# DMA transposes that read HBM scratch in place of transposes out of SBUF, in a layer of gated scan attention and quantized feed-forward

## The reference

```python
xn  = (x - mean(x)) / sqrt(var(x) + 1e-5)                 # over the 1024 features
# gated scan, all [4096, 1024]
g, v, d = xn @ Wg + bg, xn @ Wv + bv, xn @ Wd + bd
xs, a   = sigmoid(g) * tanh(v), 0.001 + 0.998 * sigmoid(d)
h[t]    = a[t] * h[t-1] + xs[t]                            # over the tokens
# feed-forward with quantized operands, INNER = 4096
aq(t) = clip(round(t * s), -128, 127) / s,  s = 127 / max|t| of the row
wq(w) = clip(round(w * s), -1, 1) / s,      s = 1 / mean|w| of the whole matrix
ff    = aq(silu(aq(xn) @ wq(w_gate).T) * (aq(xn) @ wq(w_up).T)) @ wq(w_down).T
out   = x + h + ff
```

## Time and profile before

| | us |
|---|---|
| median of 3 runs | 7357.5 (7346.43 to 7358.31) |
| the profiled execution | 7350.78 |
| its span on the slowest core (6) | 7349.2 |
| spans of all cores | 7302.0 to 7349.2 |
| PE busy | 1947.6 (27%) |
| DVE busy | 3103.3 (42%) |
| ACT busy | 396.1 (5%) |
| chain that ended last: DVE / SP's queue / DMA / PE | 39% / 26% / 11% / 11% |

### The profile page before, as it was taken

The page is one execution under the profiler, slowest core; times in us unless marked ns, Lnnn a source line. Parts: engine busy times, 40 slices in busy tenths (PEclk is TensorE's granted clock), DMA queues, the critical chain, the costliest instruction groups (busy, mean ns, idle before and its releaser), DMA issues.

```text
span 7349.2 us, 43474 instructions; the slowest of 8 cores (7302.0 to 7349.2 us)
## 1 busy us (share of the span) xinstructions
PE 1947.6 (27%) x9490; PEld 975.5 (13%) x9490; DVE 3103.3 (42%) x5413; ACT 396.1 (5%) x676; POOL 16.2 (0%) x34
## 2 busy tenths in 40 slices
PE   0031312222130000000000054435344444535656
PEld 0021212112120000000000021112121111212222
DVE  2333334242334332332423267676676767631011
ACT  1010101011010000000000000000000000000000
POOL 0000000000000000000000000000000000000000
PEclk9965656666665555555555577777777777767878
DMA  4111101011113113211311111111111111147777
GB/s 86 51 36 26 35 26 35 26 35 29 34 27 123 40 49 115 78 48 51 109 41 48 41 27 31 36 35 31 37 30 36 31 36 31 35 148 238 246 247 239
DMA packets 575298, 496.12 MB, mean 68 GB/s; under 512 B 424448, under 2 KB 440864, under 8 KB 566848
## 3 DMA queue, kind: packets, MB, share of 16 engines
q1 hardware_dynamic: 571392, 486.92, 22.2%
q0 software_dynamic: 3648, 6.41, 0.6%
HBM read 339.86 MB, written 83.89 MB: 58 GB/s over the span
## 4 chain that ended last, share of the span: by engine, by line
DVE 39%; SPq 26%; DMA 11%; PE 11%; issue 8%; ACT 2%; DVEq 2%; POOL 0%; ACTq 0%; POOLq 0%
SPq L225 23%; PE pb L715 6%; DVE qt L196 3%; DMA wqg<-scr_wdT 3%; DVE qg L208 3%; DVE qnd L206 3%; DVE qt L210 3%; DVE qnd L211 3%; DVE pbuf L629 3%; DVE qg L449 2%; DVE qg L199 2%; DVE qcm L201 2%; DVE scal L639 2%; DVE pqstage L202 2%; PE pb L379 2%
## 5 line engine op out<-in xcount | busy, mean ns | idle before, releaser
L600 PE MATMUL pb<-wqg,xqF_t 128*128 128x512 bf16 x2048 | 846.0, 413 | 1780.6 <-DMA xqF_t<-scr_xqF 1603.8
L604 PE MATMUL pb<-wqu,xqF_t 128*128 128x512 bf16 x2048 | 844.2, 412 | 0.0
L379 PE MATMUL pb<-wqu,wqg 128*128 128x256 bf16 x3072 | 388.9, 289 | 1634.4 <-DMA wqu<-pqstage 1634.4
L715 PE MATMUL pb<-wqg 128*128 128x512 bf16 x2048 | 479.4, 398 | 424.2 <-DMA wqg<-scr_wdT 424.1
L379 PEld LDWEIGHTS pb<-wqu,wqg 128*128 128x128 bf16 x3072 | 311.1, 103 | 1689.2 <-issue 1637.7
L196 DVE TENSOR_SCALAR qt<-pbuf,wsc 128x512 f32<-128x512 f32 x192 | 93.3, 486 | 1029.8 <-DMA pbuf<-wdown 339.6
L600 PEld LDWEIGHTS pb<-wqg,xqF_t 128*128 128x128 bf16 x2048 | 214.3, 105 | 2110.5 <-issue 1918.2
L397 DVE TENSOR_TENSOR epi<-epi 128x256 f32<-128x256 f32 x128 | 54.4, 425 | 818.9 <-ACT epi L394 811.7
L421 PE MATMUL pb<-scal,ones_sb 128*1 128x1 f32 x6 | 0.6, 163 | 1422.3 <-DVE scal L452 1422.3
L733 DVE TENSOR_SCALAR qt<-pb,dpwall 128x512 f32<-128x512 f32 x64 | 48.0, 751 | 743.8 <-PE pb L715 727.0
L715 PEld LDWEIGHTS pb<-wqg 128*128 128x128 bf16 x2048 | 206.2, 102 | 697.4 <-issue 483.4
(11 more groups left out here) (80 smaller groups left out, 1929.3 us busy)
## 6 DMA issues: line engine op xcount, KB each, us to landing
wqg<-scr_wdT SPq DMA_DIRECT2D x512, 256.0 KB, 5.0
pbuf<-wdown SPq DMA_DIRECT2D x64, 512.0 KB, 4.8
pbuf<-wgate SPq DMA_DIRECT2D x64, 512.0 KB, 4.6
pbuf<-wup SPq DMA_DIRECT2D x64, 512.0 KB, 4.6
scr_pqF<-pqstage SPq DMA_DIRECT2D x32, 1024.0 KB, 4.1
wqg<-scr_pqF SPq DMA_DIRECT2D x32, 1024.0 KB, 8.3
pbuf<-x SPq DMA_DIRECT2D x32, 512.0 KB, 3.5
x_grp<-x SPq DMA_DIRECT2D x32, 512.0 KB, 4.5
```

Of the source, the lines that this page charges most:

```text
L379: e.matmul(o, l, r, start=st, stop=sp),
L600: e.matmul(o, l, r, start=st, stop=sp),
L604: e.matmul(o, l, r, start=st, stop=sp),
L715: e.matmul(o, l, r, start=st, stop=sp),
```

## The change

All transposes other than those of the gate's product now read a scratch tensor in HBM and write SBUF. Four edits belong together:

- Attention: xn and xq, untransposed, are stored to scr_xn and scr_xq after quantizing (four stores). SP waits for the xn stores and issues eight transposes of scr_xn, each [256 tokens, 128 features] to 128x256. xq is not transposed here, and the eight stores of scr_xqF are gone.
- Weights: each quantized chunk is stored to scr_wd, scr_wg or scr_wu at once; there are no batches. After all three weights, SP issues eight transposes of [4096, 128] for gate and eight for up. w_down is not transposed here, and scr_wdT is gone.
- Gate/up: the eight loads of a tile's xq are transposes of [128, 128] out of scr_xq.
- Down: each of the 32 pieces of w_down per pair is a transpose of [1024, 128] out of scr_wd, so w_down is transposed anew for each of the 16 pairs.

```diff
-            for kp in range(4):
-                k = 2 * kp
-                emit_xpose4([xnbf(0 * D + k * 128, 128), ...], xnF(k * GRP, 512), src_wait=srcw)
-            for kp in range(4):
-                k = 2 * kp
-                emit_xpose4([pqstage[:, 0 * D + k * 128:0 * D + (k + 1) * 128], ...],
-                    xqF(k * GRP, 512), src_wait=srcw)
+            vq_done = wv(V)
+            for tt in range(2):
+                rows = g * GRP + tt * 128
+                op("y", lambda e, i_=xnbf(tt * D, D), o=scr_xn[rows:rows + 128, :]:
+                   e.dma_start(out=o, in_=i_), sem=SN, inc=16, wait=(vq_done,))
+                op("y", lambda e, i_=pqstage[:, tt * D:(tt + 1) * D],
+                   o=scr_xq[rows:rows + 128, :]:
+                   e.dma_start(out=o, in_=i_), sem=SX, inc=16)
...
+            for k in range(8):
+                op("y", lambda e, o=xnF(k * GRP, GRP),
+                   i_=scr_xn[g * GRP:(g + 1) * GRP, k * 128:(k + 1) * 128]:
+                   e.dma_start_transpose(o, i_), sem=TD[k], inc=16,
+                   wait=tuple(xn_rd_wait) if k == 0 else ())
...
-            for k in range(8):
-                op("y", lambda e, i_=xqF(k * GRP, GRP), o=scr_xqF[k, :, g * GRP:(g + 1) * GRP]:
-                   e.dma_start(out=o, in_=i_), sem=SX, inc=16,
-                   wait=xpose_marks_g if k == 0 else ())
...
+            for li, (src_slice, dst_rows) in enumerate(load_list):      # prep_quant
+                buf = wchunk[li % 4]
+                lp = LP[li % 4]
+                lw_ = (vmarks[li - 4],) if li >= 4 else (wv(V),)
+                op("y", lambda e, o=buf, i_=src_slice: e.dma_start(out=o, in_=i_),
+                   sem=lp, inc=16, wait=lw_)
...
+                vmarks[li] = wv(V)
+                op("y", lambda e, i_=qtmp4(li % 4, 0, D), o=dst_rows:
+                   e.dma_start(out=o, in_=i_), sem=SWs[li % 4], inc=16,
+                   wait=(vmarks[li],))
...
+        for k in range(8):
+            op("y", lambda e, o=wqg[:, k * INNER:(k + 1) * INNER],
+               i_=scr_wg[:, k * 128:(k + 1) * 128]:
+               e.dma_start_transpose(o, i_), sem=WT, inc=16,
+               wait=(st_wg + (last_attn_T,)) if k == 0 else ())
...
-                   i_=scr_xqF[k, :, i * 128:(i + 1) * 128]:
-                   e.dma_start(out=o, in_=i_), sem=lq, inc=16,
+                   i_=scr_xq[i * 128:(i + 1) * 128, k * 128:(k + 1) * 128]:
+                   e.dma_start_transpose(o, i_), sem=lq, inc=16,
...
-                op("y", lambda e, o=wbuf, i_=scr_wdT[k]: e.dma_start(out=o, in_=i_),
+                op("y", lambda e, o=wbuf, i_=scr_wd[:, k * 128:(k + 1) * 128]:
+                   e.dma_start_transpose(o, i_),
```

More of the change, by code:

```diff
@@ L51, in build_program @@
     scr_acc = nc.dram_tensor("scr_acc", [T_TOK, D], F32, kind="Internal").ap()
-    scr_xqF = nc.dram_tensor("scr_xqF", [8, 128, T_TOK], BF16, kind="Internal").ap()
+    scr_xq = nc.dram_tensor("scr_xq", [T_TOK, D], BF16, kind="Internal").ap()
+    scr_xn = nc.dram_tensor("scr_xn", [T_TOK, D], BF16, kind="Internal").ap()
     scr_pqF = nc.dram_tensor("scr_pqF", [NT, 128, INNER], BF16, kind="Internal").ap()
-    scr_wdT = nc.dram_tensor("scr_wdT", [32, 128, D], BF16, kind="Internal").ap()
+    scr_wg = nc.dram_tensor("scr_wg", [INNER, D], BF16, kind="Internal").ap()
+    scr_wu = nc.dram_tensor("scr_wu", [INNER, D], BF16, kind="Internal").ap()
+    scr_wd = nc.dram_tensor("scr_wd", [D, INNER], BF16, kind="Internal").ap()
     es = ExitStack()
@@ L139, in build_program @@
                  "LP2", "LP3", "LW4", "LW5", "LW6", "LW7",
-                 "TD0", "TD1", "TD2", "TD3", "TD4", "TD5", "TD6", "TD7",
+                 "TD0", "TD1", "TD2", "TD3", "TD4", "TD5", "TD6", "TD7", "SN", "WT",
+                 "SW1", "SW2", "SW3",
                  "SA", "SX", "SW", "SP", "SO0", "SO1"]
@@ L154, in build_program @@
         TD = [sems[f"TD{j}"] for j in range(8)]
+        SN, WT = sems["SN"], sems["WT"]
+        SWs = [sems["SW"], sems["SW1"], sems["SW2"], sems["SW3"]]
         block = es.enter_context(nc.Block())
@@ L277, in build_program @@
         act_marks = [None, None]
-        xpose_marks_g = None
+        sn_group = {}
+        mm_done_mark = None
         xg_read_done = {}
@@ L290, in build_program @@
             if g > 0:
-                op("v", lambda e: e.nop(), wait=((SA, sa_group[g - 1]), (SX, sx_group[g - 1])))
-                op("s", lambda e: e.nop(), wait=((SA, sa_group[g - 1]), (SX, sx_group[g - 1])))
+                op("v", lambda e: e.nop(), wait=((SA, sa_group[g - 1]),))
+                op("s", lambda e: e.nop(), wait=((SA, sa_group[g - 1]),))
             for tt in range(2):
@@ L298, in build_program @@
                 ln_wait = [ld_x]
-                if xpose_marks_g is not None and tt == 0:
-                    ln_wait.extend(xpose_marks_g)
+                if g > 0 and tt == 0:
+                    ln_wait.append((SN, sn_group[g - 1]))
                 op("v", lambda e, i_=xtile, o=xnb, m=meanall[:, idx:idx + 1],
@@ L313, in build_program @@
                 for pc in range(2):
-                    qw = xpose_marks_g if (xpose_marks_g is not None and tt == 0 and pc == 0) else ()
+                    qw = ((SX, sx_group[g - 1]),) if (g > 0 and tt == 0 and pc == 0) else ()
                     emit_round_neg(xnb[:, pc * 512:(pc + 1) * 512], sv,
@@ L317, in build_program @@
                                    pre_wait=qw)
-            srcw = (wv(V),)
-            for kp in range(4):
-                k = 2 * kp
[L321 to L324, removed]
-            for kp in range(4):
-                k = 2 * kp
[L327 to L331, removed]
-                    xqF(k * GRP, 512), src_wait=srcw)
+            vq_done = wv(V)
[6 more added lines that the diff above has]
+                   e.dma_start(out=o, in_=i_), sem=SX, inc=16)
+            sn_done = wv(SN)
+            sx_done = wv(SX)
+            xn_rd_wait = [sn_done]
+            if g > 0:
+                xn_rd_wait.append(mm_done_mark)
+            for k in range(8):
[3 more added lines that the diff above has]
+                   wait=tuple(xn_rd_wait) if k == 0 else ())
             xpose_marks_g = last_xpose_marks(8)
-            xn_evac_marks = xpose_marks_g
+            xn_evac_marks = tuple((TD[k], TD[k].n) for k in range(8))
             sd_mark = None
@@ L455, in qtmp4, with prep_quant @@
             return pqstage[:, cc * D + c0:cc * D + c0 + w]
-        def prep_quant(load_list, sw_col, dest4_fn, pre_first=()):
+        def prep_quant(load_list, sw_col, scr_nat, store_sem_unused, first_guard=()):
             vmarks = {}
[L459 to L485, removed]
@@ new lines, in prep_quant @@
+            store_marks = {}
+            sw0s = [wv(s4) for s4 in SWs]
+            for li, (src_slice, dst_rows) in enumerate(load_list):
[4 more added lines that the diff above has]
+                   sem=lp, inc=16, wait=lw_)
+                ldw = wv(lp)
+                for pc in range(2):
+                    pw = [ldw] if pc == 0 else []
+                    if pc == 0 and li >= 4:
+                        pw.append(store_marks[li - 4])
+                    if pc == 0 and li < 4:
+                        pw.append(sw0s[li % 4])
+                        pw.extend(first_guard)
+                    emit_round_neg(buf[:, pc * 512:(pc + 1) * 512],
+                                   wsc[:, sw_col:sw_col + 1],
+                                   qtmp4(li % 4, pc * 512, 512), clip1=True,
+                                   pre_wait=tuple(pw))
+                vmarks[li] = wv(V)
+                op("y", lambda e, i_=qtmp4(li % 4, 0, D), o=dst_rows:
+                   e.dma_start(out=o, in_=i_), sem=SWs[li % 4], inc=16,
+                   wait=(vmarks[li],))
+                store_marks[li] = wv(SWs[li % 4])
@@ L490, in build_program @@
         prep_scalars(4, 5, 1.0 / (D * INNER))
[L491 to L506, removed]
+        down_l2 = [(d_wdown[c * 128:(c + 1) * 128, q * D:(q + 1) * D],
+                    scr_wd[c * 128:(c + 1) * 128, q * D:(q + 1) * D])
+                   for c in range(8) for q in range(4)]
+        prep_quant(down_l2, 4, scr_wd, None, first_guard=((SX, sx_group[NG - 1]),))
+        st_wd = tuple(wv(s4) for s4 in SWs)
         gate_l1 = [d_wgate[c * 128:(c + 1) * 128, :] for c in range(32)]
@@ L510, in build_program @@
         prep_scalars(0, 1, 1.0 / (INNER * D))
[L511 to L518, removed]
+        gate_l2 = [(d_wgate[c * 128:(c + 1) * 128, :], scr_wg[c * 128:(c + 1) * 128, :])
+                   for c in range(32)]
+        prep_quant(gate_l2, 0, scr_wg, None)
+        st_wg = tuple(wv(s4) for s4 in SWs)
         up_l1 = [d_wup[c * 128:(c + 1) * 128, :] for c in range(32)]
@@ L522, in build_program @@
         prep_scalars(2, 3, 1.0 / (INNER * D))
[L523 to L530, removed]
+        up_l2 = [(d_wup[c * 128:(c + 1) * 128, :], scr_wu[c * 128:(c + 1) * 128, :])
```

(14 more changed lines are left out.)

6 lines of the change are left out of this document (4 added, 2 removed).

## The result

The changed kernel takes 6726.2 us (median of 8 runs) where the kernel before takes 7355.1 us on the same chip: a ratio of 0.9147, 95% interval 0.913 to 0.9164. It is 629 us faster; 957 us were forecast. 6726 us lies inside the range given (6150 to 7600 us), but just above the forecast's own range, without the rivals (6230 to 6720 us). The profiled execution has a span of 6723.9 us on core 6, the core that was also the slowest before.

A forecast was written before the change was run, and what follows sets the result against it. Bound by SP's queue, each SBUF transpose holding it 1.232 us. 7350.8 - 571 (attention) - 595 (weights) + 78 (gate and up transposes) + 0 (gate/up) + 131 (down) = 6394; with 6.7 added, 6400 us; range 6150 to 7600.

The forecast's parts named there:

- The term for gate and up: After all quantizing: sixteen transposes of 4096x128, 16.8 MB at 222 GB/s plus the last store, adding 78 us.
- Rival (a): All transposes: the queue's price goes by 128x128 block whatever the source; about 11,800 us in all; chance 0.17.
- Rival (c): Down stage: longer waits for weights keep TensorE's clock at the lower level; 275 us more, 6675 us; chance 0.06.
- Rival (b): Transposes from HBM: not queue-bound, but slower than the share says, say 110 GB/s; 7087 us; chance 0.17.
- X: Time a transpose reading HBM holds SP's queue: bracketed by 0.432 us and 1.232 us per block, taken as 0.54 us.
- the +160: Gate/up stage: cost over 32 tiles if each xq transpose holds the queue 1.232 us; the forecast itself took 0.
- +131: Down stage: transposing w_down anew for each of 16 pairs makes a pair 59.8 us against 51.6, adding 131 us.
- so a packet of 256 bytes costs the DMA engines the same transposed or not: DMA rate: transposes scaled to 217 GB/s at full share and plain xqF loads to 225, so 222 was taken.
- R: Delivery rate of a transpose reading HBM: bracketed by 26 and 286 GB/s, taken as 222 GB/s.
- the issue, 32 x 0.54 = 17 us, is hidden behind them: Down stage, per pair: issuing 32 transposes takes 17 us, hidden behind the 37.8 us transfer of w_down.
- 595: Weights: a chunk takes 11.4 us against 17.4 and the 32 stores of scr_wdT go, saving 595 us.
- another 500: Weights: had loads been free to run ahead, VectorE's 6.0 us a chunk would limit, saving another 500 us.

The follow-up runs named there:

- The ladder: Down-stage means of the kernel before and variants of the changed kernel's w_down loads: plain 2 KB rows 823 us, plain 256-byte contiguous 981, transposed contiguous 1072, transposed at 8 KB pitch 1104 to 1123.

## Why the prediction was right in sign and too high in size

The mechanism was right: the kernel waited for SP's queue in the transposes, fewer instructions there bring the time back, and what is bought is paid for in part by loads that no longer run ahead and by w_down's transposes in the down stage. The term for gate and up (+78, measured 84.6) held. Rival (a), a price by block, fell: the down stage is 1145 us, not 5400. Rival (c) fell: the granted clock rose from 0.79 to 0.82 there, and TensorE waited for the pieces of w_down, 656 us in 293 waits. Rival (b) had the right direction: the scaled rate was too high, but the 198 GB/s of transposes by themselves are nearer to the 222 taken than to its 110.

The first step that failed is X, "8 x 0.54". I had bracketed the price between a plain load's 0.432 us and 1.232 us per block, and took a value near the plain load (below even the 0.61 us of the average plain load there), since the block price seemed to belong to SBUF sources. The third reading of the earlier trace rows was missing: 1.232 us for the instruction, out of SBUF or HBM, and not eight times as much for eight blocks. The row had shown it with one size only, so it could not tell a price by block from a price by instruction, and for a tile's xq, of one block each, the two give the same number: the +160 that stood in the text as the upper bound (measured +182.6 on core 6, 175 in the mean; plain loads brought it all back). In attention the eight issues took 10.18 us for 4.3, 5.9 us more. In 16 groups that is 94, of which 72 are seen in the stage: the sum had set a whole landing behind the eighth issue, but it is counted from where that issue starts (342.87 above), 1.2 us less a group. The Trainium skill's statement ("DMA: Bandwidth & Descriptors", section "Why a DMA increments its semaphore by 16 and not by 1") that an HBM transpose costs 631 cycles per instruction, "small tiles", agrees with the runs in that the price is per instruction for 1, 2 and 8 blocks. That it would be well below that of a transpose out of SBUF, as I read from it, they do not show: 1.10 us at least for either.

The second is the down stage, +317 for +131, and there the step "so a packet of 256 bytes costs the DMA engines the same transposed or not". The ladder takes it apart. Plain loads in such rows cost 158 to 173 us, not far from the 131 of the sum; the rest of what was missing came with the transposing (+92) and with the pitch under it (+32 to 51). The rows of the stage say the same, scaled to a full share as the prediction did: 245/0.76 = 322 GB/s before, 201/0.80 = 251 for plain pieces of 256 bytes, 177/0.85 = 208 for transposed ones. The first step down is a factor of 1.28, which agrees with the 27% overhead that the Trainium skill ("DMA: Bandwidth & Descriptors", section "Why small descriptors are slow (HBM only)") gives for descriptors of 256 bytes. The prediction was right to call that in the price already; the second step down is what it left out. Its R of 222 GB/s came from scaling two light loads (26 GB/s at 0.12, 54 at 0.24) to a full share, where by themselves the transposes of gate and up reached 198, 11% less than 222. A share printed with two digits at a tenth of the load is a loose base. And X failed here too: "the issue, 32 x 0.54 = 17 us, is hidden behind them". The 32 issues of a pair took 56.24 us. Even at 1.26 us each they are 40 us, more than the 37.8 of the transfer that was to hide them. How much of the +92 is the queue and how much the DMA engines stays open.

The third went the other way. The weights gained 708 for 595: 39 us because a batch before took 71.1 us on average (1707 us for 24), not the 69.5 of the batch I read, and 74 nearly all because w_gate's and w_up's chunks land a microsecond sooner, which w_down's row could not show. The added wait was as described: 11.4 us a chunk for w_down, to the tenth, and its removal brought 432 us where "another 500" stood.

So the 332 us between the two sums (957 and 625) are +183 (gate/up), +186 (down), +72 (attention), +7 (transposes of gate and up), and -113 (weights), -2 (statistics). That the weights gave back more than forecast, for reasons that the sum did not have, is luck: without it the forecast would have been off by 445 us.

## What to carry to other kernels

A duration seen at one size says nothing of how it grows: bracket it by block, by byte and by instruction, and work the sum out for each. If the price is per instruction, as it nearly was up to eight blocks here, make the instructions large: lay the scratch out so that one transpose fetches what eight did. And where a store that waits is put on the queue that also prefetches, issue the next loads first; here that order alone was worth 432 us in its stage, two thirds of what the whole change brought. And before calling a queue's work hidden, multiply the price of one issue by their number and set it beside the transfer. A transpose whose result is needed many times is paid for once, in a stage where the queue is idle.

## What the runs showed of the hardware

- A DMA transpose held SP's queue for 1.1 to 1.26 us as a rule, out of SBUF (1 block of 128x128) or HBM (1, 2 or 8 blocks); one of 16 blocks for 1.81 us, one of 8 blocks just behind a 1 MB store for 1.96, and one of 32 blocks, the DMA engines full, for 4.9. A plain load of one such block, or one in 128 rows of 2 KB, held it for 0.32 to 0.43 us, but a plain load in 1024 rows of 256 bytes for 1.12 in the down stage (medians).
- Transposes of [4096, 128] back to back were delivered at 198 GB/s on the profile's core, with the DMA engines full; stores in rows of 2 KB reached 349 GB/s in the kernel before at the same share (2872.2 to 2893.0 us).
- 134 MB of w_down read in pieces of 256 bytes in place of 2 KB cost 158 us more, transposing them another 92, and a row pitch of 8 KB another 32 to 51 on the transposed loads; on plain ones 15 us, which is within the scatter.
